# A four-layer graph network on one core: the second layer's entry in chunks, its adjacency normalised, its batch-norm scales inside reflections

## What is computed

```
h = relu(layernorm(x));  x = x + L0(h, adj)    # normalised adjacency, W1, batch norm, relu, W2, batch norm
h = relu(layernorm(x));  x = x + L1(h, adj)
h = relu(layernorm(x));  x = x + L2(h, adj)    # U, U^T from eigh of a normalised Laplacian of adj, two dense layers
h = relu(layernorm(x));  x = x + L3(h, adj)    # three dense layers, each times adj*adj

def L1(x, adj):
    h = relu(adj @ (x @ Wg0 + bg0))
    h = relu(adj @ (h @ Wg1 + bg1))
    for p in 1..4:                   # windows of p nodes, an LSTM over each, its last state
        h[:, idx_p] = lstm_p(windows(h, p))
    return h
```

## Time and profile before

| | us |
|---|---|
| median of 3 runs | 991.04 (990.54 to 991.86) |
| the profiled execution: its own time | 989.27 |
| its span | 987.5 |
| TensorE busy | 848.7 (86%) |
| VectorE busy | 578.6 (59%) |
| ScalarE busy | 522.6 (53%) |
| GpSimd busy | 342.9 (35%) |

### The profile page before, as it was taken

One profiled execution on the slowest core, in us unless ns is written; L12 is line 12 of the kernel. 1 busy time (PEld: TensorE's weight loads), 2 busy tenths in 40 slices (PEclk: granted clock), 3 DMA queues, 4 the chain that ended last, 5 costly groups with the idle time before them and its releaser, 6 DMA issues.

```text
span 987.5 us, 12462 instructions
## 1 busy us (share of the span) xinstructions
PE 848.7 (86%) x3721; PEld 566.4 (57%) x3721; DVE 578.6 (59%) x3094; ACT 522.6 (53%) x962; POOL 342.9 (35%) x412
## 2 busy tenths in 40 slices
PE   2678668489999988998799868778999999999998
PEld 1444323264577546774378434566758848848846
DVE  5799867789878896779989985005104204304101
ACT  0466457358656737566466634464554554544531
POOL 1333100206555645565657646662202202202000
PEclk9999979789999999998899989998999999999999
DMA  8000000000000000000000000000000100100101
GB/s 339 0 1 1 1 0 1 1 1 1 1 1 1 1 1 2 1 1 1 0 1 1 1 0 1 0 1 1 1 0 2 43 0 2 43 0 1 43 1 43
DMA packets 2963, 13.34 MB, mean 14 GB/s; under 512 B 464, under 2 KB 464, under 8 KB 2640
## 3 DMA queue, kind: packets, MB, share of 16 engines
q1 hardware_dynamic: 2896, 12.54, 3.2%
HBM read 8.35 MB, written 4.19 MB: 13 GB/s over the span
## 4 chain that ended last, share of the span: by engine, by line
PE 64%; DVE 26%; POOL 4%; ACT 3%; issue 2%; DMA 0%; SPq 0%; DVEq 0%; ACTq 0%; POOLq 0%
PE PS L439 63%; POOL BIG L951 2%; DVE ST L1619 2%; DVE stats L1591 2%; DVE Fq L1410 1%; DVE seg L1411 1%; DVE X L1759 1%; DVE mv L1598 1%; POOL sc L931 1%; ACT T L782 1%; DVE sc L1144 1%; DVE vcol L1141 1%; ACT BIG L871 1%; DVE sc L1219 1%; DVE S L1161 1%
## 5 line engine op out<-in xcount | busy, mean ns | idle before, releaser
L439 PE MATMUL PS<-BIG,wts 128*128 128x512 f32 (+2 forms) x952 | 343.7, 498 | 10.7 <-POOL BIG L951 7.9
L951 POOL TENSOR_TENSOR BIG<-BIG 128x256 f32<-128x256 f32 (+2 forms) x252 | 238.0, 951 | 185.9 <-ACT BIG L871 115.9
L439 PEld LDWEIGHTS PS<-BIG,wts 128*128 128x128 f32 x952 | 178.9, 193 | 133.8 <-issue 97.7
L871 ACT ACTIVATE BIG<-PS,lbias 128x256 f32<-128x256 f32 (+2 forms) x312 | 165.7, 559 | 108.8 <-PE PS L439 107.3
L439 PE MATMUL PS<-H,wts 128*128 128x256 f32 (+2 forms) x312 | 120.1, 488 | 17.7 <-POOL BIG L951 7.2
L1759 DVE TENSOR_TENSOR X<-X,PS 128x512 f32<-128x512 f32 x64 | 43.4, 682 | 129.5 <-PE PS L439 87.1
L774 ACT ACTIVATE BIG<-PS 128x1024 f32<-128x1024 f32 x64 | 65.5, 1024 | 88.5 <-PE PS L439 88.5
L774 ACT ACTIVATE T<-PS 128x512 f32<-128x512 f32 x96 | 55.9, 594 | 94.7 <-PE PS L439 94.7
L439 PE MATMUL PS<-T,wts 128*128 128x512 f32 x192 | 99.6, 642 | 1.4 <-ACT T L774 1.1
L782 ACT ACTIVATE T<-X,shift,rstd 128x128 f32<-128x128 f32 x192 | 78.5, 482 | 36.2 <-DVE shift L1607 36.2
L1786 DVE TENSOR_TENSOR T<-PS,wts 128x512 f32<-128x512 f32 x16 | 11.1, 692 | 143.8 <-PE PS L439 143.8
(11 more groups left out here) (309 smaller groups left out, 1254.6 us busy)
## 6 DMA issues: line engine op xcount, KB each, us to landing
X<-x_in SPq DMA_DIRECT2D x1, 4096.0 KB, 12.6
out<-X SPq DMA_DIRECT2D x16, 256.0 KB, 2.0
wts<-w_in SPq DMA_DIRECT2D x1, 3605.5 KB, 20.7
cst<-cst_in SPq DMA_DIRECT2D x1, 419.0 KB, 3.5
AA<-adj_in SPq DMA_DIRECT2D x2, 16.0 KB, 2.0
```

The costliest lines, as they stand in the source:

```text
L439: return nc.tensor.matmul(o, l, r, start=start, stop=stop)
L871: nc.scalar.activation(LB[:, q, {"i": I_, "g": G_, "f": F_, "o": O_}[g], 0:n], PS[:, 3 * q + rank[q] % 3, 0:n], ACT.Tanh if g == "g" else ...
L951: nc.gpsimd.tensor_tensor(out, a, b, op).then_inc(pool_set[q], 1)
```

## The change

1. **Normalised adjacency.** Two new matrices, made once beside reflection 3: `BDP`, the adjacency with each row divided by its sum, and `BDR`, the adjacency times the row sums. Since the sums are positive, `relu(adj @ (x Wg0 + bg0))` is the row sum times `relu(rownorm(adj) @ x Wg0 + bg0)`; `agg` uses `BDP`, and the factor is in `BDR`. So bg0 is one number per feature, and ScalarE adds it with the ReLU, straight from PSUM (`relu0`). `bias0`, 16 VectorE instructions, and `RB0` go. `g0` is one product of 512 columns, `g1` four of 128, and `agg2` comes last, followed by the one `bias` on VectorE.
2. **A wave.** For the first group all engines go through the entry in an order sorted by planned times (`LEAD_IN`), chunk after chunk; VectorE has it among its reflections, which begin at once. The last ReLU of this group is on GpSimd (L995 of the new kernel).
3. **Batch-norm scales.** `bn_scales` stands in the waits of reflection 21 and of the last one, with its roots on GpSimd (`bn_roots`), ahead of that reflection's own root.
4. **Constant products.** TensorE does 12 products of the identity with itself (`warm`) ahead of the first `turn`, and 12 ahead of the first `agg`; nothing reads them.
5. **Roots of the third layer** (`last_stats`): for the last group on VectorE, among the chain's last steps, and no more on GpSimd.
6. A sigmoid of one column at ScalarE's start. `SLOWED`, `PACE_TWIST`, `BEGINS` and the first due time have other values, by which small products stand elsewhere.

```diff
         return self.before + len(self.steps)
 
 
-GRAPH = ["agg", "g0", "agg2", "g1"]
+GRAPH = ["agg", "g0", "g1", "agg2"]
 C_PE = Order(B_PE.end, [(0, n) for n in ["turn"] + GRAPH]
              + [(j, n) for i in range(ITER) for j, names in ((i + 1, ["turn"]), (i - 1, ["turn_h"]), (i + 1, GRAPH))
                 if 0 <= j < ITER for n in names])
-C_ACT = Order(B_ACT.end, [(i, n) for i in range(ITER) for n in ["bn", "norm", "aggT", "relu0", "aggT2", "h"]])
-C_DVE = Order(B_DVE.end, [(0, n) for n in ["add"] + LN + ["bias0", "bias1"]]
-              + [(j, n) for i in range(ITER) for j, names in ((i + 1, ["add"]), (i - 1, ["add_h"]), (i + 1, ["bias0", "bias1"]))
+C_ACT = Order(B_ACT.end, [(i, n) for i in range(ITER) for n in ["bn", "norm", "aggT", "relu0", "g1T"] + ["h"] * (i > 0)])
...
 
 DVE_STEP = {"reflect": 0.24, "grid": 0.16, "twist": 0.27, "tail": 0.21}
 
-SLOWED = 1.06
+SLOWED = 1.08
 
 ROUND_TRIP = 0.8
 
-BEGINS = 6.0
+BEGINS = 0.5
 
 PASS = 2.1
 
 LN_STEP = 0.5
 
-GAP = 0.5
-
-STARTED = 10.0
+LEAD_IN = {"bn": (0.0, 0.75), "turn": (1.0, 0.75), "add": (2.0, 2.0), "shift": (5.4, 2.0), "norm": (5.6, 2.0),
+           "agg": (7.4, 2.2), "aggT": (8.6, 2.3), "g0": (9.4, 2.4), "relu0": (10.5, 2.5), "g1": (11.3, 2.6),
+           "g1T": (12.5, 2.6), "agg2": (13.3, 2.6), "bias": (14.5, 2.6)}
+
+
+def lead_in(*names):
+
+
+    return sorted((LEAD_IN[n][0] + LEAD_IN[n][1] * k, n, k) for n in names for k in range(NK))
...
+            def warm(n):
+
+
+                for _ in range(n):
+                    mm(task_bank[:, 0:P], ident, ident)
+
             pe.wait_ge(hh_S, REFLECTED + 1)
             old_row(eb(0)[:, (REFLECTED % 2) * NODES:], REFLECTED).then_inc(hh_row, 1)
+            warm(WARM)
...
                     m.then_inc(pe_done[k], 1)
                 elif name == "agg":
                     pe.wait_ge(act_done[k], C_ACT.at(j, "norm"))
-                    tiles(o, k, T0[:, k, :], BDAT[:, :])
+                    tiles(o, k, T0[:, k, :], BDP[:, :])
                 elif name == "g0":
                     pe.wait_ge(act_done[k], C_ACT.at(j, "aggT"))
-                    tiles(o, k, T1[:, k, :], W("wg0"))
-                elif name == "agg2":
+                    mm(o, W("wg0"), T1[:, k, 0:CH]).then_inc(pe_done[k], 1)
+                elif name == "g1":
                     pe.wait_ge(act_done[k], C_ACT.at(j, "relu0"))
-                    tiles(o, k, T0[:, k, :], BDAT[:, :])
+                    tiles(o, k, T0[:, k, :], W("wg1"))
                 else:
-                    pe.wait_ge(act_done[k], C_ACT.at(j, "aggT2"))
-                    mm(o, W("wg1"), T1[:, k, 0:CH]).then_inc(pe_done[k], 1)
...
                         if 1 in todo:
                             task(*todo[1])
 
-            for name in ["turn"] + GRAPH:
-                for k in range(NK):
-                    if name == "agg":
-
-                        pe.wait_ge(dve_done[k], C_DVE.at(0, "add"))
-                    product(0, name, k, l1_bank(k))
-                spend(STARTED if name == "turn" else GAP)
+            for at, name, k in lead_in("turn", *GRAPH):
+                clock[0] = max(clock[0], at)
+                if name == "agg":
+                    if k == 0:
+                        warm(WARM)
+                        pe.wait_ge(prep_dve, PREP["biases"])
+
...
 
+            act.wait_ge(ld_cst, 16)
+            nc.scalar.activation(scratch[:, :], C("half"), ACT.Sigmoid)
...
                 elif name == "g0":
-                    act.wait_ge(dve_done[k], C_DVE.at(i, "bias0"))
-                    nc.scalar.activation(T0[:, k, :], T1[:, k, CH:2 * CH], ACT.Relu).then_inc(act_done[k], 1)
-                elif name == "g1":
-                    act.wait_ge(dve_done[k], C_DVE.at(i, "bias1"))
+                    copy(k, T0[:, k, :], b, C_PE.at(i, "g0"), ACT.Relu, bias=W("bg0"))
+                elif name == "agg2":
+                    act.wait_ge(dve_done[k], C_DVE.at(i, "bias"))
                     nc.scalar.activation(by_tile_of_set(i, k),
                                          T1[:, k, CH:2 * CH].rearrange("p (t m) -> p t m", t=TPC), ACT.Relu)\
                         .then_inc(act_done[k], 1)
 
-            for k in range(NK):
-                bn(0, k)
-            for k in range(NK):
-                norm(0, k)
-            for name in GRAPH:
-                for k in range(NK):
-                    after(0, name, k, l1_bank(k))
+            for at, name, k in lead_in("bn", "norm", "aggT", "relu0", "g1T"):
+                if name == "bn":
+                    bn(0, k)
+                elif name == "norm":
+                    norm(0, k)
+                else:
+                    after(0, {"aggT": "agg", "relu0": "g0", "g1T": "g1"}[name], k, l1_bank(k))
             for i in range(ITER):
...
 
+            def bn_roots(groups, at, seen, n):
+                x, y = lnv[:, 0, 0:groups], lnv[:, 1, 0:groups]
+                pool.wait_ge(bn_var, seen)
+                nc.gpsimd.tensor_scalar(x, bnv[:, at + 1:at + 2 * groups:2], EPS, None, ALU.add).then_inc(bn_root, 1)
+                pool.wait_ge(bn_root, n + 1)
+                nc.gpsimd.tensor_tensor(y, x, mh[:, 0:groups], ALU.pow).then_inc(bn_root, 1)
+
             for r in range(REFLECTED):
+                if r == LEAD + L0_FIRST:
+                    bn_roots(2, 0, 2, 0)
+                if r == REFLECTED - 1:
+                    bn_roots(1, 10, 3, 2)
                 pool.wait_ge(hh_norm2, r + 1)
                 root(sc[:, 36:37], sc[:, 3:4], C("half")).then_inc(hh_norm, 1)
...
                 layer_norm_roots(0, k, C_POOL, C_DVE)
+            for k in range(NK):
+                pool.wait_ge(dve_done[k], C_DVE.at(0, "bias"))
+                nc.gpsimd.tensor_scalar(by_tile_of_set(0, k), T1[:, k, CH:2 * CH].rearrange("p (t m) -> p t m", t=TPC),
+                                        0.0, None, ALU.max).then_inc(pool_done[k], 1)
             for i in range(ITER):
                 for r, (p, s, part) in enumerate(LSTM):
-                    if i == ITER - 1 and r == LAST_ROOTS:
-                        for k in range(NK):
-                            layer_norm_roots(0, k, D_POOL, D_DVE)
                     for q in range(2):
                         place, n = lstm_in(H(i), q, p, s, part)
...
-                ins.then_inc(bn_ops, 1)
+                yield
                 dve.wait_ge(bn_ops, nb[0])
-
-            def bn_scales(st, groups, g, be, at, ready):
-
-                for c in range(groups):
-                    bstep(v.bn_aggr(b1(at + 2 * c, 2), st(c)))
-                means, var = bnv[:, at:at + 2 * groups:2], bnv[:, at + 1:at + 2 * groups:2]
-                scale, shft = b1(at + 2 * groups, groups), b1(at + 3 * groups, groups)
-                x, y, a = (lnv[:, q, 0:groups] for q in range(3))
-                bstep(v.tensor_scalar(x, var, EPS, None, ALU.add))
-                for f in inverse_root(x, y, bstep, lambda: None):
-                    bstep(v.tensor_tensor(a, y, y, ALU.mult))
-                    bstep(v.tensor_tensor(a, a, x, ALU.mult))
-                    bstep(v.scalar_tensor_tensor(y, a, -f, y, ALU.add, ALU.mult))
-                bstep(v.scalar_tensor_tensor(scale, y, -1.0 / 8192, g, ALU.mult, ALU.mult))
-                bstep(v.tensor_tensor(shft, means, scale, ALU.mult))
-                bstep(v.tensor_tensor(shft, be, shft, ALU.subtract))
-                v.sem_inc(ready, 1)
+                v.tensor_tensor(shft, means, scale, ALU.mult).then_inc(bn_ops, 1)
+                nb[0] += 1
+                yield
+                dve.wait_ge(bn_ops, nb[0])
...
-                    step(v.tensor_scalar(RB0[:, :], W("bg0row"), c1(0), None, ALU.mult))
+                    step(v.tensor_scalar(tmp[:, :], PS[:, 1, 0:P], TINY, None, ALU.max))
+                    step(v.reciprocal(tmp[:, :], tmp[:, :]))
+                    step(v.tensor_tensor(BDP[:, :], BDAT[:, :], tmp[:, :], ALU.mult))
+                    step(v.tensor_scalar(BDR[:, :], BDAT[:, :], c1(0), None, ALU.mult))
                     step(v.tensor_scalar(RB1[:, :], PS[:, 1, 0:P], W("bg1"), None, ALU.mult))
                     step(v.tensor_tensor(lbias[:, :], W("bih"), W("bhh"), ALU.add), "biases")
+                beside = [] if n < 0 else [l0_first(n)] if n < L0_FIRST else [l0_second(n - L0_FIRST)]
                 if n == L0_FIRST:
-                    dve.wait_ge(hidden_seen, 2 * NCHUNK)
-                    bn_scales(lambda c: ST1[:, c, :, :].rearrange("p n s -> p (n s)"), 2, W("g1"), W("be1"), 0, bn1_ready)
-                beside = iter(()) if n < 0 else l0_first(n) if n < L0_FIRST else l0_second(n - L0_FIRST)
+                    beside = [hidden_scales()] + beside
...
+                    yield from norm_roots(do, wait, later)
+                    for k in range(NK):
+                        v.scalar_tensor_tensor(shift[:, k, :], mv[:, k, :, 0], -1.0, rstd[:, k, :], ALU.mult, ALU.mult)\
+                            .then_inc(dve_done[k], 1)
```

(22 more changed lines are left out.)

177 lines of the change are left out of this document (106 added, 71 removed), and 4 rows, old and new, of the table TASKS.

## The result

The changed kernel takes 991.75 us (median of 16 runs), the kernel before 989.66 on the same occasions: a ratio of 1.0026 (95% interval 1.0014 to 1.0037), about 2.6 us slower. The ratio takes in all runs and lies above that of the medians (1.0021), since twelve of the sixteen took 990.2 to 992.3 us at a mean granted clock of 0.962 to 0.965, and four took 996.0 to 996.7 us at 0.954 to 0.957. The forecast was 971.5, within 961 to 983; it started from 991.04 for the kernel before, 1.4 us above the 989.66 measured here. The profiled execution took 990.58 us in 988.8 us of span.

A forecast was written before the change was run, and what follows sets the result against it. It took TensorE to bound the LSTM groups and a chain over the engines the second layer's entry; +1.8 −2.9 −4.4 −0.5 −3.0 −6.6 −6.8 +3.0 = −19.4 off 991.04 gave 971.6, stated as 971.5, range 961 to 983 us.

The forecast's parts named there:

- Item 1: Beside reflection 3: VectorE's extra work for the new matrices is hidden by nothing, +1.8 us (1.4 to 2.2).
- Item 2: First batch-norm scales: their own stretch on VectorE goes, some work enters the reflection, −2.9 us (−3.5 to −1.5).
- Item 3: Second layer's entry: first gates at 216.2 instead of 220.63, −4.4 us (bounds −11 and +1.4).
- Item 4: First gates: the sigmoid table load moves to ScalarE's idle start, −0.5 us (−2.2 to 0).
- Item 5: LSTM groups: TensorE's waits for `S` shrink with biases off VectorE and products asked later, −3.0 us (−6 to +2).
- the waits stay: LSTM: waits for `S` and `both_ways` stay as they are, 9.6 us of gain lost, 981 us; chance 0.20.
- Item 6: LSTM: the `both_ways` wait falls from 7.7 to 3.2 us and the half clock goes, −6.6 us (−9.8 to 0).
- Item 7: Round 7: GpSimd's roots ahead of its products go, and TensorE's wait with them, −6.8 us (−7 to −4).
- Item 8: Last `EV` product: eight of the moved root steps on VectorE add to its wait, +3.0 us (+1.4 to +9.9).
- blocked rival: VectorE's eight root steps each meet a GpSimd product, 9.9 us rather than 3.0, 978.5 us; chance 0.10.
- Everything else is at nothing: Outside the listed terms: transfers, third and fourth layer and the sigmoid at the start change nothing.
- slower rival: Entry: the four chunks don't overlap and TensorE stays at half clock, +9 us, near 999; chance 0.03.

The follow-up runs named there:

- padded: Changed kernel with twelve VectorE instructions of 128 x 512, read by nothing, where the twelve biases of groups 2 to 4 had stood: 992.07 us, ratio 1.0036.
- old_due: Changed kernel with the kernel before's two planning numbers (SLOWED 1.06, PACE_TWIST 32.5): 985.27 us, ratio 0.9960.
- no_const: Changed kernel without the 24 constant products of the entry: 989.65 us, ratio 0.9995.
- old_due_no_const: Changed kernel with SLOWED 1.06 and PACE_TWIST 32.5 and without the 24 constant products: 980.17 us, ratio 0.9911.
- slowed_no_const: Changed kernel with SLOWED 1.06 (PACE_TWIST stays 37) and without the 24 constant products: 986.17 us, ratio 0.9957.
- before_roots: Kernel before with one part of the change alone, the roots of the third layer's first norm on VectorE: 982.67 us, ratio 0.9934.
- roots_back: Changed kernel with the roots of the third layer's first norm on GpSimd again, ahead of round 7's products: 1002.43 us, ratio 1.0123.

## Why the prediction was wrong, step by step

**Item 1, +1.8.** GpSimd's root of the fourth reflection, the first behind the new steps, is at 32.15 instead of 30.65: +1.5. At the twentieth only 0.6 of it is left in this pair of executions (116.44 for 115.88), but that is scatter: on average over the five traces that have the old first layer and the twelve that have the new one, the fourth root is 1.6 us later and the twentieth 1.4. Right.

**Item 2, −2.9.** The product of the reflection behind the first scales moves from 130.91 to 128.38; with the 0.6 of item 1 in this pair that is −3.1. Right.

**Item 3, −4.4.** By items 1 to 3 the gates were to come 5.5 us earlier; they came 5.1 earlier. First `agg` at 194.97, forecast 195.7. The sum by rows held, with the cost of the constant products in it (1.5 us forecast through the late add, 1.7 measured).

**Item 4, −0.5.** The first gate activation gained 1.9 us more than the gates, of which 1.3 was lost again by the eighth: −0.6. Right.

**Item 5, −3.0 for `S`.** This step failed. The waits are 5.2 us where they were 5.1. They do not go with how much work VectorE has had by then: `padded` adds 8 us of it and they stay. Nor does asking later by itself shorten them: one of these products (the one of 64 x 11) stands behind 292 records of LSTM products on TensorE in the kernel before, behind 296 in the changed one and 300 in `old_due`, and the waits are 5.1, 5.2 and 6.2 us. The rival "the waits stay" was right in this part. Between n = 24 and 104 another 3.3 us are lost. `old_due` loses 3.0 there, `no_const` 4.7, but `old_due_no_const` and `slowed_no_const` only 0.9. All of these have the new order of the graph products, so that order can't be what costs the 3.3; SLOWED and the constant products change it together. Why they do stays open.

**Item 6, −6.6 for `both_ways`.** The wait shrank as forecast (4.1 for 3.2). The clock did not hold, though: 0.83 from 580 to 600 us, so the −2.1 for it was wrong. The larger fault is that the same number with the other SLOWED only exchanges this wait for one on a bank.

**Item 7, −6.8.** From n = 280 to 292, 6.8 us are gained, in the changed kernel and in `before_roots`; in the whole it is 10.7 (loosely) by `roots_back` and 6.4 by `before_roots`, with item 8 in both. Right.

**Item 8, +3.0.** This term was mis-sized: 0.5 in the changed kernel, nothing in `before_roots`. I charged eight steps at their mean time and forgot that the chain waited for TensorE there, 2.33 us before `EV<-EV,PS` in the kernel before. The blocked rival did not come about.

**What was missing, the main fault.** The sum had terms for what SLOWED and PACE_TWIST do to TensorE's small products, and wrote "the due times put each small product about 3 us of TensorE's work later" as a gain. It had none for what the same clock does to VectorE's order: which steps of the layer stand ahead of which steps of the chain. I had the fourth group's stretch in the trace (TensorE idle 4.83 us at 486 for GpSimd, beside the passes), left it under "Everything else is at nothing", and compared orders only at the entry and at the end. The order of the changed kernel showed, before any run, that `rstd` and `shift` had moved behind both passes of 128 x 2048. By rows of the kernel before that was 2 x 2.29 us, and more where the clock falls.

The profiled executions differ by +1.3 us where the sum said −19.4. Of the 20.7 us between, 5.0 were lost from n = 184 to 192 with the roots behind the passes (12 when they are moved there in `old_due`). From 192 to 224, 5.8 were lost; `old_due` and `old_due_no_const` lose 3.7 there against the kernel before, so most of it comes with the new structure, and which part of that was not tried. Items 5 and 6 fell short by 6.3 and 3.6. From 252 to 274, 4.2 were lost where `old_due` gains 3.0; but `old_due` loses 3.7 from 224 to 252, where the changed kernel gains 3.0. Over both stretches the two lie 0.6 us apart (+1.3 and +0.7 against the kernel before), so item 6's gain was mostly handed back a few rounds later. The forecast was kinder than needed in item 8 by 3.0 from n = 280 to 292, and after the last scan the changed kernel gains 1.9 us more, where I had put nothing. The rest, 0.5, is in items 1 to 4 and between n = 104 and 184.

**The slower rival.** I gave slower 0.03 by a mechanism in the entry that did not occur. A program whose orders all come from a few numbers has places where two steps can change sides; the numbers tried here were worth 3 to 9 us, the roots alone 12, and every other pair of numbers tried in the kernel before made it slower. That is a reason from this trace for a wide range on the slow side, and the prediction had none.

## What to carry to other kernels

When a change moves a number that sets more than one engine's order, compare the orders over the whole program, not only where the change has its purpose, and look first where a short step that others wait for stands beside long ones: a shift of 0.17 us that got behind two passes of 2.29 us, with the roots ahead of it, cost up to 12 us. Retune such numbers after each structural edit and test each part with the old ones too; here the new structure with the old numbers and without the constant products is 0.9% faster than the kernel before, and the new numbers and the constant products took all of it back. Most of that 0.9% is the move of the last roots, which alone gave 0.7%. A wait that is removed by asking later is only gone if nothing on either engine stands behind it.
